# Attention kernel: score chunks of equal width, and the output projection of step 2 placed between the scores

## The reference

```python
xn = _layernorm(x, axis=-1)
q, k, v = heads(xn @ Wq.T), heads(xn @ Wk.T), heads(xn @ Wv.T)
q, k = _rmsnorm(q, q_norm_w), _rmsnorm(k, k_norm_w)
scores = einsum('bkgqd,bksd->bkgqs', qg, k) / sqrt(128)
attn = softmax(scores + where(rel > 0, -1e30, slopes * rel), axis=-1)
s = (einsum('bkgqs,bksd->bkgqd', attn, v) as b, s, 32*128) @ Wo.T
g = silu((silu(xn @ w_gate.T) * (xn @ w_up.T)) @ w_down.T)
out = x + s * g
```

## Time and profile before

| what | value |
|---|---|
| median of 3 runs | 2482.01 us (2481.6 to 2482.16) |
| profiled execution, its own time | 2481.58 us |
| its span, first to last instruction | 2479.7 us |
| TensorE busy | 2432.2 us, 98% |
| VectorE busy | 1680.3 us, 68% |
| ScalarE busy | 1234.7 us, 50% |
| GpSimd busy | 778.2 us, 31% |
| granted TensorE clock, mean | 0.996 |
| DMA | 92.19 MB, mean 37 GB/s |

### The profile page before, as it was taken

How to read it: one execution, slowest core, us unless ns; L and a number is a source line. 1 busy time by engine, 2 the same in 40 slices (tenths; PEclk the granted TensorE clock), 3 DMA queues, 4 the chain that set the end, 5 groups by cost and what they waited for, 6 DMA issues and landing times.

```text
span 2479.7 us, 37446 instructions
## 1 busy us (share of the span) xinstructions
PE 2432.2 (98%) x13232; PEld 2063.4 (83%) x13232; DVE 1680.3 (68%) x3709; ACT 1234.7 (50%) x2548; POOL 778.2 (31%) x2154
## 2 busy tenths in 40 slices
PE   6999999999999999999989999999999999999998
PEld 5888888888888888788878888888888888887887
DVE  5777777777868687723267777777777777777132
ACT  3555554555545555533345555555554555545333
POOL 4323241413233223144533232323231414231443
PEclk9999999999999999999999999999999999999999
DMA  3000000000000000023320101010000000010223
GB/s 125 5 27 18 26 18 26 18 26 18 26 18 26 18 27 18 26 78 135 110 77 1 43 1 43 1 36 8 26 18 26 18 26 18 1 43 14 90 96 108
DMA packets 22841, 92.19 MB, mean 37 GB/s; under 512 B 6528, under 2 KB 6656, under 8 KB 18560
## 3 DMA queue, kind: packets, MB, share of 16 engines
q1 hardware_dynamic: 22656, 89.80, 10.5%
HBM read 85.60 MB, written 4.19 MB: 36 GB/s over the span
## 4 chain that ended last, share of the span: by engine, by line
PE 95%; DVE 2%; ACT 1%; issue 1%; DMA 0%; POOL 0%; SPq 0%; DVEq 0%; POOLq 0%; ACTq 0%
PE score_ps L325 16%; PE out_ps L349 16%; PE out_ps L362 14%; PE qkv_ps L299 14%; PE ring_ps L336 10%; PE qkv_ps L300 7%; PE score_ps L432 5%; PE qkv_ps L432 5%; PE ring_ps L447 3%; PE ring_ps L307 2%; PE out_ps L447 1%; PE ring_ps L312 1%; PE score_ps L299 0%; DMA qkv_raw<-w_qkv_dram 0%; DVE y L838 0%
## 5 line engine op out<-in xcount | busy, mean ns | idle before, releaser
L518 ACT ACTIVATE pT_hi<-ring_ps 128x512 fp32r<-128x512 f32 x576 | 343.8, 599 | 524.1 <-PE ring_ps L336 512.9
L694 DVE TENSOR_TENSOR pT_lo<-ring_ps,pT_hi 128x512 fp32r<-128x512 f32 x576 | 395.9, 689 | 91.8 <-ACT pT_hi L518 88.1
L510 ACT ACTIVATE probs<-probs,low_min 128x896 f32<-128x896 f32 (+7 forms) x512 | 394.7, 772 | 44.8 <-DVE low_min L686 44.5
L857 POOL TENSOR_SCALAR rs_x<-sq_sum 128x5 f32<-128x5 f32 x128 | 25.3, 198 | 1134.5 <-DVE sq_sum L654 1134.5
L336 PE MATMUL ring_ps<-ident,probs 128*128 128x128 f32 x2304 | 347.2, 274 | 1.0 <-DVE probs L704 1.0
L686 DVE CUSTOM_DVE_ANT_0 probs<-score_ps,rel_sb,slope 128x512 f32<-128x512 f32 (+3 forms) x512 | 329.7, 645 | 8.9 <-PE score_ps L325 5.6
L336 PEld LDWEIGHTS ring_ps<-ident,probs 128*128 128x128 f32 x2304 | 278.6, 141 | 51.2 <-issue 1.6
L325 PE MATMUL score_ps<-kv_hi,qT_hi 128*128 128x512 f32 (+3 forms) x768 | 278.5, 363 | 12.0 <-DVE kv_lo L672 6.4
L349 PE MATMUL out_ps<-pT_hi,kv_hi 128*128 128x512 f32 x576 | 266.1, 462 | 2.4 <-DVE pT_lo L694 2.0
L325 PE MATMUL score_ps<-kv_hi,qT_lo 128*128 128x512 f32 (+3 forms) x768 | 266.7, 347 | 0.0
L325 PE MATMUL score_ps<-kv_lo,qT_hi 128*128 128x512 f32 (+3 forms) x768 | 265.1, 345 | 0.0
(11 more groups left out here) (136 smaller groups left out, 5411.5 us busy)
## 6 DMA issues: line engine op xcount, KB each, us to landing
qkv_raw<-w_ffn_dram SPq DMA_DIRECT2D x44, 768.0 KB, 4.2
qkv_raw<-w_qkv_dram SPq DMA_DIRECT2D x16, 1536.0 KB, 6.7
o_raw<-w_o_dram SPq DMA_DIRECT2D x16, 1024.0 KB, 4.8
probs<-x_dram SPq DMA_DIRECT2D x4, 1024.0 KB, 7.2
o_raw<-x_dram SPq DMA_DIRECT2D x4, 1024.0 KB, 6.5
out_dram<-y SPq DMA_DIRECT2D x16, 256.0 KB, 3.8
rel_sb<-rel_dram SPq DMA_DIRECT2D x1, 512.0 KB, 11.3
inv_slope<-inv_slopes_dram SPq DMA_DIRECT2D x16, 2.5 KB, 1.7
```

What stands on the lines that cost most here:

```text
L510: act.activation(row, row, ACT.Exp, scale=-1.0, bias=low_min[:, i % 2, h, HEAD_CHUNKS[i] - 1:HEAD_CHUNKS[i]], accum_out=row_sum[:, i % 2, ...
L518: act.activation(pT_hi[:, n % SLOTS, :], ring_ps[:, ring_bank(r), :], ACT.Copy).then_inc(ring_high, 1)
L694: dve.tensor_tensor(out=pT_lo[:, n % SLOTS, :], in0=ring_ps[:, ring_bank(r), :], in1=pT_hi[:, n % SLOTS, :].bitcast(F32), op=ALU.subtract) ...
```

## The change

The chunks of a tile get equal widths: tile 4 has 320+320 keys instead of 512+128, tile 5 384+384 instead of 512+256, tile 6 448+448 instead of 512+384; tile 7 keeps 512+512, tiles 0 to 3 their one chunk. TensorE's scores and DVE's bias use the new bounds. Their number, order and semaphores stay.

And `spread` now holds in step 2 as well, in the units that aren't first of their row (U % UNITS > 0, 14 of 16). There the output projection of tile 0 is cut as in step 1: heads 0 and 1 before the loop, head 2 after slot 0's transpositions, head 3 after slot 1's, and DVE's add_y moves from before the loop to the end of slot 1.

```diff
 HEAD_CHUNKS = [-(-(i + 1) * P // BANK) for i in range(TILES)]
+CHUNK_WIDTH = [(i + 1) * P // HEAD_CHUNKS[i] for i in range(TILES)]
...
# in scores (TensorE) and in bias (DVE)
-                lo, hi = part * BANK, min((part + 1) * BANK, (i + 1) * P)
+                lo, hi = [(part + end) * CHUNK_WIDTH[i] for end in range(2)]
...
# in step of TensorE and in step of DVE
-                spread = i == 1 and not first
+                spread = i == 1 and not first or i == 2 and U % UNITS > 0
```

## The result

The changed kernel takes 2489.5 us (median of 8 runs, 2486.1 to 2490.8), the kernel before 2482.1 us: a ratio of 1.0028, 95% interval 1.0018 to 1.0037. It is slower by 7.4 us. The profiled execution took 2487.03 us (span 2485.1).

The account below looks back on a forecast made before the run. TensorE, busy 98% of the span with 95% of the chain, was taken as the bound. Terms -7.4 + 0.6 + 0.4 + 0.5 + 11.9 = +6.0 us on 2482.0 gave 2488.0 us, range 2482.5 to 2493.0.

Parts of the forecast that it names:

- the mechanism that was given the largest chance: Step 2's added wait outweighs what equal chunks save in step 4: slower, 2488.0 us, chance 0.78.
- tile 4, 320+320: Step 4's scores: equal chunks avoid the slow 128-column group, saving 0.46 us per unit, -7.4 us.
- tile 5, 384+384: Scores of tile 5: 1.06 us per head instead of 1.05, over 64 heads +0.6 us.
- tile 6, 448+448: Scores of tile 6: 1.23 us per head before and after, 0.
- last steps of a batch: Steps 6 and 7 of each batch's last unit: longer last chunks uncovered by a QKV projection, +0.4 us in 2 units.
- near misses in step 4: First weigh and score chunk 5 have only 0.02 and 0.04 us of cover against VectorE: charged +0.5 us.
- step 2: The spread projection makes the first weigh wait for add_y, net +0.85 us per unit, 14 units, +11.9 us.
- The wait in step 2: First weigh waits 1.02 us: chain through low_probs 1 and add_y takes 2.68 us, TensorE's work beside it 1.66.
- The floor of narrow matmuls: Score matmuls on TensorE: a 128-column group takes 0.28 us, not the straight line's 0.18.
- the interpolation to 320 columns: Step 4's scores: a 320-column group lies midway between 256 and 384 columns, 0.44 us.
- Rival B: Step 2: the weigh starts without any wait, so the kernel gets faster, 2473.7 us; chance 0.10.
- What the profile would show: Step 2's weigh about 1.2 us behind score 2's last matmul, released by VectorE's y; step 4 shorter by 0.43 to 0.46.

Follow-up runs that it names:

- widths alone: The kernel before with equal chunk widths only, step 2 not spread: 2475.1 us, ratio 0.9973.
- 384+256: The kernel before with equal chunk widths except tile 4 in 384+256 keys, step 2 not spread: 2475.3 us, ratio 0.9974.
- 448+192: The kernel before with equal chunk widths except tile 4 in 448+192 keys, step 2 not spread: 2481.1 us, ratio 0.9998.
- add_y first: The changed kernel with VectorE issuing add_y before low_probs 1 in step 2: 2478.2 us.
- both repairs: The changed kernel with, in step 2, add_y before low_probs 1 on VectorE and score chunk 3 before the first weigh on TensorE: 2472.3 us.
- the spread alone: The kernel before with the projection spread in step 2 and the old chunk widths: 2495.9 us, ratio 1.0053.
- POOL's split moved: The changed kernel with POOL splitting v before the norms in step 2 instead of behind them: 2488.8 us.

## Why the prediction was right, point by point

The forecast of 2488.0 us (+6.0) met 2489.5 (+7.4), slower as said, by the mechanism that was given the largest chance. Its terms against the profiled executions:

| term | predicted | measured |
|---|---|---|
| tile 4, 320+320 | -7.4 | 16 x -0.45 = -7.2 |
| tile 5, 384+384 | +0.6 | 14 units x 0.03 = +0.4 |
| tile 6, 448+448 | 0 | 14 units, -0.3 in sum |
| last steps of a batch | +0.4 | widths alone: +0.06 in the first batch's stretch that holds them |
| near misses in step 4 | +0.5 | none |
| step 2 | 14 x 0.85 = +11.9 | +12.2 |
| sum | +6.0 | +5.2, or +5.4 with all else |

- **The wait in step 2** was right in place, size and cause. The chain from the transpositions to the weigh was put at 2.68 us and measured 2.67, the wait at 1.02 and measured 1.00; turning add_y and low_probs round took 0.53 us out of the window, moving POOL's work took nothing. Rival B, a wait that is hidden, falls with the 13.05 us of step 2.
- **The floor of narrow matmuls** was right, and the interpolation to 320 columns too (0.43 to 0.44 us a group against 0.44; 0.45 us saved per unit against 0.46). 384+256 and 448+192 show that it is a floor and not a matter of equality.
- **Too cautious** were two small terms, together 0.9 us: the margins of 0.02 and 0.04 us in step 4 held (the step lost the whole 0.45), and the longer last chunk cost nothing measurable even where no projection covers it.
- **What the profile would show** was wrong in one point: I wrote that the wait would be released by VectorE's y. It was, but the profile put it down to POOL's kv_lo, which ends 0.07 us later by accident. I hadn't asked what else ends near the forecast time.
- **What the sum lacks**: the profiled executions differ by 5.4 us, the medians by 7.4. The profiled execution is among the changed kernel's fastest; the remaining 2 us go with the mean clock of the others (last section). Step 3's +0.7 wasn't in the forecast at all. So that +6.0 lies between the terms' sum and the medians' difference is partly luck: too much for the small terms, nothing for step 3 and the clock.

## What to carry to other kernels

When a block of work is cut up and moved between others, its consumer on another engine moves too: write down the chain from the last piece to whoever needs its result, with the in-order queue between them, and compare it with the work that is left beside it. Here that chain, on an engine that was 68% busy, cost 14 waits of 1 us on the engine that sets the time. With two lines of VectorE turned round the idle time falls from 0.83 to 0.29 us, and with only one head moved, behind slot 0, step 2 is 0.14 us shorter than unspread. And a releaser named by a profile is only the last event before the start: look which semaphore the waiting instruction names and up to which count, and move the suspect to be sure.

## What the runs showed of the hardware

**The clock between executions.** The times of the changed kernel's 8 executions go with the mean granted clock: 2486.1 us at 0.997, 2487.0 at 0.996, 2488.6 to 2490.8 at 0.995. For the kernel with add_y first it is 2476.3 to 2478.5 at 0.997 and 2482.9 to 2485.3 at 0.993 and 0.994. Before a change of under 0.2% is read from a median, the mean clocks have to be compared: the kernel before had 0.995 or 0.996 in all of its runs beside these. The traces show single stretches at the lower level of 1.2 GHz (a granted clock of 0.50). Windows of 5 us at the end of the first batch, the kernel before:

```profile
1045.00:1050.00 5.00, 2.85 (x12) 2.01 (x11) 3.17 (x7) 1.72 (x3) 0.00 (x0) 0.95 0.02 2
1050.00:1055.00 5.00, 4.37 (x20) 3.43 (x20) 2.75 (x5) 1.57 (x3) 0.00 (x0) 0.71 0.00 0
```

and within the second of them:

```profile
1050.00:1052.00 2.00, 2.00 (x6) 1.52 (x6) 0.90 (x2) 0.00 (x0) 0.00 (x0) 0.50 0.00 0
```

The same place in the changed kernel:

```profile
1050.00:1055.00 5.00, 3.01 (x14) 2.46 (x15) 3.52 (x6) 1.21 (x3) 0.00 (x0) 1.00 0.02 2
1055.00:1060.00 5.00, 4.37 (x31) 3.64 (x29) 3.27 (x5) 3.23 (x6) 0.03 (x1) 1.00 0.00 0
```

Both follow a window in which TensorE was busy only 2.9 to 3.0 of 5 us; in one execution the clock fell, in the other not. The kernel with both repairs had one such stretch more in its profile:

```profile
1005.00:1010.00 5.00, 3.19 (x14) 2.24 (x13) 2.85 (x9) 3.27 (x7) 2.80 (x7) 0.94 0.51 187
1010.00:1015.00 5.00, 5.00 (x21) 4.05 (x21) 3.90 (x9) 0.42 (x1) 0.00 (x0) 0.72 0.35 133
```

What such a stretch costs can be read from all eleven traces. From the last step 5 of the first batch to the next batch's first matmul of `project` it takes 253.3 to 253.4 us in the six that have none there (the changed kernel's among them), 254.9 to 255.0 in the four that have one (the kernel before, the widths alone, 384+256, 448+192), and 256.4 with both repairs, where there are two. From the last step 5 of the second batch to the end it takes 258.7 to 258.8 us, and 260.2 to 260.3 in the three traces that have one more there (the spread alone, POOL's split moved, 448+192). So each costs about 1.5 us, whatever the kernel.

At the start the changed kernel's trace has the lower level for longer: from 34 to 41 us the granted clock is 0.51, in the kernel before 0.76. 448+192, with 0.52 there, is also late at the first step 2, by 0.7 us against 1.0. Most of the changed kernel's executions have a mean of 0.995, where the kernel before has 0.995 or 0.996. Of the executions at 0.995 there is no trace, so where the clock falls in them, and whether the change or chance decides it, stays open.
